# Expert weights loaded during the first batch, and a stacked operand of four buffers, in a kernel of random-feature attention and a routed FFN

## The reference, cut to what matters

```python
q, k, v = (x @ W.T + b).reshape(B, L, 16, 8)            # for Wq, Wk, Wv
p = einsum('blhd,dm->blhm', q_or_k, proj_mat) / sqrt(8)
q_prime, k_prime = concat([cos(p), sin(p)], -1) / sqrt(128)
kv = einsum('blhm,blhd->bhmd', k_prime, v)
out = einsum('blhm,bhmd->blhd', q_prime, kv)
x = layernorm(x + out @ Wo.T + bo)
logits = x @ Wr + br                                     # 8 experts, best 2
h = relu(x @ W1[e] + b1[e]);  y_e = h @ W2[e] + b2[e]
x = layernorm(x + sum_e routed[e] * y_e)
```

## Time and profile before

| | us |
|---|---|
| median of 3 runs | 612.55 (609.89 to 614.1) |
| the profiled execution | 608.14 |
| its span, first to last instruction | 606.3 |

### The profile page before, as it was taken

One profiled execution on the slowest core, in us unless ns is written; L12 is line 12 of the kernel. 1 busy time (PEld: TensorE's weight loads), 2 busy tenths in 40 slices (PEclk: granted clock), 3 DMA queues, 4 the chain that ended last, 5 costly groups with the idle time before them and its releaser, 6 DMA issues.

```text
span 606.3 us, 13845 instructions
## 1 busy us (share of the span) xinstructions
PE 494.6 (82%) x4206; PEld 311.4 (51%) x4206; DVE 433.2 (71%) x1106; ACT 397.9 (66%) x489; POOL 390.0 (64%) x400
## 2 busy tenths in 40 slices
PE   4089198999999989999999989876999999999100
PEld 2054034434444434444444444465999999999100
DVE  1478277789898967897898988514677777777273
ACT  2069156978979849889889889422556666665274
POOL 2024573989989957978989896715345555555384
PEclk9579688999999979999999999855899999999655
DMA  3213522222223231232222224603222222221572
GB/s 68 84 66 121 148 94 74 102 83 100 101 89 114 82 105 53 99 104 88 94 89 84 102 98 109 209 0 86 69 68 71 70 70 70 70 70 50 151 206 71
DMA packets 57111, 55.77 MB, mean 92 GB/s; under 512 B 6647, under 2 KB 49257, under 8 KB 57065
## 3 DMA queue, kind: packets, MB, share of 16 engines
q1 hardware_dynamic: 52713, 46.16, 24.3%
q0 software_dynamic: 4352, 8.99, 4.5%
HBM read 37.16 MB, written 17.97 MB: 91 GB/s over the span
## 4 chain that ended last, share of the span: by engine, by line
PE 44%; POOL 20%; issue 10%; DVE 7%; DMA 7%; SPq 5%; ACT 4%; POOLq 0%; ACTq 0%; DVEq 0%
PE ang L694 11%; PE misc L703 10%; PE misc L549 5%; POOL routed_dram L1283 5%; POOL feats L1215 4%; PE ang L494 3%; DMA parts_dram<-parts 3%; PE misc L514 3%; SPq L361 3%; POOL qk_f L309 2%; DVE turns L929 2%; PE ang L485 2%; DVE feats L937 2%; POOL parts L313 2%; DMA bo_bc<-attn_bo 2%
## 5 line engine op out<-in xcount | busy, mean ns | idle before, releaser
L929 DVE TENSOR_SCALAR turns<-ang 128x1024 f16<-128x1024 f32 x128 | 155.5, 1218 | 67.4 <-PE ang L485 41.7
L754 ACT ACTIVATE feats<-ang 128x1024 f32<-128x1024 f32 x128 | 131.8, 1030 | 88.5 <-PE ang L494 86.5
L1215 POOL TENSOR_TENSOR feats<-feats 128x1024 f32<-128x1024 f32 x56 | 108.9, 1946 | 66.8 <-ACT feats L755 66.4
L755 ACT ACTIVATE feats<-ang 128x1024 f32<-128x1024 f32 x128 | 131.7, 1029 | 0.0
L827 ACT ACTIVATE feats<-weights_mem 128x1156 f32 x72 | 82.9, 1165 | 54.1 <-DVE feats L1162 41.4
L1301 POOL DMA_INDIRECT expert_dram<-feats x72 | 69.3, 962 | 75.5 <-DVE feats L1157 73.0
L937 DVE TENSOR_TENSOR feats<-feats 128x1024 f32<-128x1024 f32 x72 | 102.0, 1417 | 0.7 <-ACT feats L755 0.6
L1283 POOL DMA_INDIRECT routed_dram<-rows_s,slots x64 | 80.9, 1263 | 18.8 <-issue 18.3
L494 PE MATMUL ang<-turns,negi 128*128 128x512 f16 x256 | 78.6, 389 | 6.1 <-DVE turns L929 5.1
L549 PE MATMUL misc<-feats,kv_pad 128*32 128x512 f32 x512 | 70.3, 618 | 15.1 <-POOL feats L1215 12.7
L694 PE MATMUL ang<-feats 128*128 128x128 f32 x576 | 78.0, 279 | 0.0
(11 more groups left out here) (153 smaller groups left out, 613.1 us busy)
## 6 DMA issues: line engine op xcount, KB each, us to landing
weights_mem<-parts_dram SPq DMA_DIRECT2D x64, 288.0 KB
parts_dram<-parts SPq DMA_DIRECT2D x16, 384.0 KB, 8.9
feats<-routed_dram SPq DMA_DIRECT2D x72, 65.0 KB, 1.8
feats<-expert_dram SPq DMA_DIRECT2D x16, 256.0 KB, 3.6
x_in<-attn_x SPq DMA_DIRECT2D x8, 256.0 KB, 14.3
x_all<-attn_x SPq DMA_DIRECT2D x8, 256.0 KB, 5.2
weights_mem<-ffn_W SPq DMA_DIRECT2D x8, 256.0 KB, 4.9
out<-feats SPq DMA_DIRECT2D x8, 256.0 KB, 2.4
```

The source lines that it names most:

```text
L754: act.activation(f[:, 0, :], a, ACT.Sin, scale=TWO_PI)
L755: act.activation(f[:, 1, :], a, ACT.Sin, scale=TWO_PI / 2).then_inc(s["sines"], 1)
L929: dve.tensor_scalar(turns[:, u % 2, :], ang[:, slot(ph, u), :], MAGIC, -MAGIC, ALU.add, ALU.add)\
L1215: pool.tensor_tensor(f, f, f, ALU.mult).then_inc(s["sq_p"], 1)
```

## The change

- `stk` gets memory of its own, with four buffers (one for each head group) that both sides use in turn. A read of a head group now waits for the `angles` of the same head group on the other side, eight units back, where it was sixteen.
- The loads of W1, W2, b1 and b2 move from the end of SP's queue (and from among the small loads) to `load_rest`, together with `x_all` and the small loads. `load_rest` stands in batch 0 between the write of side 1 and its four reads.
- `expert_biases` moves into batch 0: b1 is turned in unit 2, two experts each are done in units 4, 5, 9 and 10, in PSUM bank `misc[:, 1]`; ACT's copies come in units 2, 5 and 10. `project(0, 1, 1)` and the first `out_product` wait for the copies.
- The exponential and the gates come after the first eight tiles.

```diff
-EARLY = HG * G * LEN // 2 // WROW
+EARLY = EXP // 2
-        stk = weights_mem[0:STK, 0:HG * G * LEN].bitcast(BF16).rearrange("p (s a g n) -> p s a g n", s=2, a=HG, g=G)
+        stk = sb("stk", [STK, HG, G, LEN], BF16)
-        def tile_steps(eng, steps):
+        def tile_steps(eng, steps, then=None):
             steps(0, True, False)
+            if then:
+                then()
                 def read(side, hg):
-                    hold(sp, "angles", UNITS, b, HALF * side + 2 * hg + 2 - UNITS)
+                    hold(sp, "angles", UNITS, b, 2 * hg + 2 - HALF * (1 - side))
                 for side in range(2):
                     write(side)
+                    if side == 1 and isinstance(b, int) and b == 0:
+                        load_rest()
                     for hg in range(HG):
                         read(side, hg)
+            def load_rest():
+                for dst, src in ((b1_raw[:, :], b1.rearrange("e (j p) -> (e j) p", p=P)), (b2_s[:, :], b2)):
+                    sp.dma_start(dst, src).then_inc(s["b_in"], 16)
+                for x_e in range(EXP):
+                    sp.dma_start(experts[:, x_e, AT_W2:AT_B2].rearrange("p (j d) -> p j d", j=HT),
+                                 W2[x_e].rearrange("(j p) d -> p j d", p=P)).then_inc(w2_in[x_e // EARLY], 16)
+                for t in range(BATCH):
+                    sp.dma_start(x_all[:, t * LT:(t + 1) * LT, :], x_rows[t]).then_inc(s["xload"], 16)
...
+                for lo in (0, EARLY):
+                    sp.dma_start(experts[:, lo:lo + EARLY, 0:HID], W1[lo:lo + EARLY].rearrange("e d h -> d e h"))\
+                        .then_inc(s["w1_in"], 16)
+            def turn_b1():
+                pe.wait_ge(s["b_in"], 32)
+                pe.wait_ge(s["v_ev"], 1)
+                pe.transpose(misc[:, 1, 0:EXP * HT], b1_raw[:, :], ident[0:EXP * HT, 0:EXP * HT]).then_inc(s["b1_mm"], 1)
+            BIASES = {4: (0, 2), 5: (2, 4), 9: (4, 6), 10: (6, 8)}
+                    if first and u == 2:
+                        turn_b1()
+                    if first and u in BIASES:
+                        expert_biases(*BIASES[u])
-            expert_biases(0, EXP // 2)
             rows_T(e - 1, "y_ok", 1, e, 0)
             logits(e - 1, "xr_ev", 1, e, 0)
             ranks(e - 1, "lg_ok", 1, e, 0)
-
-            expert_biases(EXP // 2, EXP)
```

More of the change, by code:

```diff
@@ L46 @@
 N_LOADS = 6
-N_WLOADS = 11
+N_WLOADS = 9
 N_SETUP = 9
@@ L358, in _ @@
             load_x(1)
             stack(0)
[L360 to L367, removed]
@@ L377, in _ @@
             sp.dma_start(routed_dram[EXP * REGION:EXP * REGION + P, :], pad_rows[:, :]).then_inc(s["pads_in"], 16)
[L379 to L385, removed]
             sp.wait_ge(s["pads_at"], 1)
@@ L485, in angles @@
                         mm = pe.matmul(a[:, t * 512:(t + 1) * 512], proj_stk[:, :],
-                                       stk[:, 1, hg, 2 * half + t, :], start=True, stop=False,
+                                       stk[:, hg, 2 * half + t, :], start=True, stop=False,
                                        skip_group_check=True)
@@ L780, in _, with bias_evac, b1_evac @@
             proj_evac(0, 1, 0)
+            def bias_evac(h):
+                act.wait_ge(s["b2_mm"], h + 1)
+                act.activation(experts[:, h * EARLY:(h + 1) * EARLY, AT_B2:AT_B1],
+                               misc[:, 1, :].rearrange("p (e d) -> p e d", e=EARLY), ACT.Copy).then_inc(s["b2_ok"], 1)
+            def b1_evac():
+                act.wait_ge(s["b1_mm"], 1)
+                b1_T = misc[:, 1, 0:EXP * HT]
+                act.activation(experts[:, :, AT_B1:WROW], b1_T.rearrange("p (e j) -> p e j", e=EXP), ACT.Copy,
+                               scale=-1.0)
+                act.activation(b1_s[:, :], b1_T, ACT.Copy).then_inc(s["b1_ok"], 1)
             def body(b, ph):
@@ L785, in body @@
                 for u in range(UNITS):
+                    if first and u == 2:
+                        b1_evac()
+                    if first and u in (5, 10):
+                        bias_evac(u // 10)
                     if u == 3 and not first:
@@ L799, in _ @@
             out_evac(BATCH - 1)
-            act.wait_ge(s["b1_mm"], 1)
-            b1_T = banks[5][:, 0:EXP * HT]
-            act.activation(experts[:, :, AT_B1:WROW], b1_T.rearrange("p (e j) -> p e j", e=EXP), ACT.Copy,
-                           scale=-1.0)
-            act.activation(b1_s[:, :], b1_T, ACT.Copy).then_inc(s["b1_ok"], 1)
             normalize(BATCH - 1)
@@ L810, in _ @@
             keep_rows(BATCH - 1)
-            for h in range(2):
-                act.wait_ge(s["b2_mm"], h + 1)
-                act.activation(experts[:, h * EXP // 2:(h + 1) * EXP // 2, AT_B2:AT_B1],
-                               banks[3 + h].rearrange("p (e d) -> p e d", e=EXP // 2), ACT.Copy)\
-                    .then_inc(s["b2_ok"], 1)
-            act.wait_ge(s["gap_ok"], 1)
-            act.activation(gate[:, 1, :], gate[:, 0, :], ACT.Exp).then_inc(s["gap_exp"], 1)
             act.wait_ge(s["w1_in"], 32)
-            act.wait_ge(s["b2_ok"], 2)
             act.wait_ge(s["tab_ok"], 2)
@@ L1179, in _ @@
             x_evac_tile(0, 1)
-            tile_steps(dve, steps)
+            tile_steps(dve, steps, gates)
             for n in range(BATCH):
```

70 lines of the change are left out of this document (39 added, 31 removed).

## The result

| | before | after |
|---|---|---|
| median, 4 runs each | 611.22 us (606.94 to 614.1) | 626.32 us (624.85 to 635.94) |
| profiled execution | 608.14 | 627.17 |
| span | 606.3 | 625.3 |

The ratio is 1.0245, 95% interval [1.0161, 1.0329]: 15 us slower. The predicted 620.0 had the sign right and half the size (+7.5).

What follows compares the result with a forecast made beforehand. PE was taken as nearly always busy, with gaps in batch 0 and the passage from attention to experts. +12.8 at unit 8 of batch 1 less 5.3 in the passage made +7.5, so 612.55 became 620.0 us; range 611 to 628.

Steps and rivals of the forecast that it cites:

- a slower batch 1: Part of the forecast's own range: units 0 to 7 of batch 1 in 20.2 to 24.8 us, -0.7 to +3.9.
- rival 4: Passage: scatter or its landing, not `rows_T`, sets the first tile, so no 5.3 us gain; +12.8, 625.4 us; chance 0.06.
- if the passage keeps its length: Sign against the forecast: the passage from attention to experts is not shortened, where 5.3 us less was claimed.
- Unit 8 of batch 1 (+12.8): Batches 0 and 1: side 1 reads behind the loads and added expert products make this unit start 12.8 us later, at 121.3.
- first wait: Batch 0, behind unit 2: PE waits 9.6 us for b1, until 45.5; hidden by the later wait at unit 8.
- The passage (-5.3): Attention to experts: four experts' bias products leave the way of `rows_T`, which starts earlier; 5.3 us less.
- The gates (0, at most 1.5): Expert tiles: exponential and gates behind the first eight tiles cost 0, at most 1.5 us if PE stood throughout.
- The ring and the place of the loads at the end (0): Later batches and the end: four buffers leave a margin of about 6 us, PE does not wait for loads; 0.
- Rival 3: Each batch: the ring is too short, first side 1 read 1.8 us late; some 10 us over seven batches, 630; chance 0.10.
- Rival 1: Batch 0: side 1 reads get through by 65, not held up by the loads; -3.8 us, 608.8 us; chance 0.17.
- Rival 2: Batch 0: all loads go at W1's rate, 354 GB/s; +3.3 us, 615.9 us; chance 0.12.

Runs made afterwards that it cites:

- before_again: The kernel before, nothing edited, run once more for a second profile; 610.52 us.
- after_again: The changed kernel, nothing edited, run once more; 626.21 us, ratio 1.0222 to before.
- biases_split: Against the kernel before: two bias products ahead of `rows_T`, one ahead of the ranks, five behind; 615.35 us over 10 runs, ratio 0.9983.
- gates_back: Against the changed kernel: exponential and gates ahead of the tiles again; 624.58 us, ratio 1.0237 to before.
- b2_only: Against the kernel before: each expert's bias product cut to its first matmul, leaving out W2 times b1; 612.83 us over 10 runs, ratio 0.9947.

## Why the prediction was right in part

The measured 626.32 lies in the range of 611 to 628, near its top. In part that is luck: the range reached up there for a slower batch 1, the gates and the spread of the runs, of which only the gates came, and not for a passage that gives nothing, which had 0.06 as rival 4. By its own test ("if the passage keeps its length") the forecast failed in that term.

*Unit 8 of batch 1 (+12.8): right.* +12.2 in its own terms, +14.2 against before_again, whose unit 8 came 2.0 us earlier. The steps hold one by one: first wait ended at 44.44 (45.5 predicted), W1 issued at 61.56 (61.6), unit 8 at 73.61 (74.0), batch 1's first units in 20.3 (20.9). The rates taken from the last batch held roughly: 266 to 285 GB/s while W2 and `x_all` moved (253 and 268 taken), 376 for W1 in 64 to 68 us (354). Behind unit 8 of batch 1 nothing was foreseen, and the executions differ there: +12.1 at batch 7 in after, +16.5 in after_again.

*The passage (-5.3): the step that failed.* "Four experts leave the way of `rows_T`. It can start at 395.95 instead of 400.92". That is what the one trace showed, and after against that trace did gain it (34.9 to 29.5). But the 2.72 us for an expert were those of an execution whose clock had fallen at 390.7, 2.1 us behind the start of the product with Wo (388.55) and inside the first expert's product. biases_split is the only other profile like that. In every other profile with four products in this place they took 1.50 us each. The measured term is +0.4 (29.1 to 29.5). The earlier trace rows had the sign of it: clock 0.80 in 388 to 392.5 us, in a stretch full of work. In before_again the product with Wo comes 7.1 us later, and the window that is as far from it reads

```profile
395.00:399.50 4.50, 3.41 (x22) 2.82 (x23) 1.94 (x9) 0.84 (x3) 2.43 (x5) 1.00 0.80 296
```

(The prediction names this hole slices 25 to 28; the digits of the earlier trace rows have it in 26 to 28, which are the 379 to 424 us that it gives.)

The price of that step is rival 4's, +12.8 and 625.4 us, close to the 626.32 measured, but not by its mechanism: neither the scatter nor its landing changed.

*The gates (0, at most 1.5): too low.* "ACT copies weights ahead of PE in four buffers there and has idle time, DVE 103.5 of 134". The busy share said that there is slack; whether DVE is ahead of PE at a pass head was not asked. Measured: 3.6 us between the means of the two groups of profiles (+3.9 in after, +0.4 in after_again), 6.3 in the medians where it was the only edit (615.0 to 621.3; the interval of the ratio is 0.8 to 14 us), and nothing seen in the time of gates_back. So the sign is clear and the size is not.

*The ring and the place of the loads at the end (0): right*, 0.9995. Rival 3 is out. Rival 1 is out: unit 8 waited until 73.61. Rival 2 is out by the rates above.

In sum, after against before_again: +14.2 at batch 1, -2.1 up to batch 7, -0.8 up to Wo, +0.4 in the passage, +3.9 in the tiles: +15.6. after_again has +12.8, +3.7, -1.1, +0.4 and +0.4: +16.2. The medians have 15.1. What repeats is the first term, as forecast, and a passage that gives nothing. Most of the missing half of the forecast is that 5.3; the other 2 to 3 us stand in different places in the two executions.

The page "DMA: Bandwidth & Descriptors" of the Trainium skill, section Bandwidth, gives the 341 GB/s for a transfer of 1 MB, and the prediction weighed it for all loads. Here W2 and `x_all`, in transfers of 256 KB, moved at 266 to 285 GB/s, below it, and the two 1 MB transfers of W1 at 376 in 64 to 68 us, above it.

## What to carry to other kernels

A load costs what stands behind it in its queue, not what it feeds: ask for each stretch of the queue when it is idle, and put early loads there (8 to 20 us here: 13 us gained), instead of where they are merely early enough. Before work is moved off a chain, look at what it lies beside and at the clock in that stretch; where another engine's wait ends at the same time, moving it gains nothing, and costs its full duration where it lands. And take a second profile of the kernel before, and of the one after: two stretches of the first, of 5 to 6 us each and of opposite sign, were not those of the usual execution.

## What was not expected of the hardware

- The execution to execution difference lies in few places: units 0 to 7 of batch 5 took 19.9 us in one profile of before and 25.5 in another, of the same code; and PE's clock fell at 390.7 us in the one and 408.8 in the other. Batch 5 has a wait of 2.36 us and then PE at 1.2 GHz for some 7 us. The batch 7 of after_again that took 4.3 us more has the same two things (waits of 2.12 and 1.81 us, then the lower clock from 374.0). What sets either was not found.
- Taking some 12 us of matmuls away from a stretch of 29 us (b2_only) did not shorten it in the profile (30.2 us); the median fell by 2.8 us.
- Eight DMAs of 256 KB issued at 7.74 us held SP until 20.92, 1.65 us each, and the write behind them went out only 1.5 us later (21.97 for 20.45).
